# Where the factors' hi and lo parts, the power and a slice's lo part stand in the quads of a Flamingo block kernel

## What is computed

```python
x = x + tanh(g_xattn[0]) * xattn(layernorm(x), ctx, ctx, Wq, Wk, Wv, Wd)   # 32 heads, 8 kv heads, DK = 128, causal
x = x + tanh(g_ffn[0]) * ffn(layernorm(x), ...)

def anemll_linear(x, w, su, sv):       # gate, up (512 -> 1792) and down (1792 -> 512), rank of su @ sv is 4
    w_eff = w * (su @ sv)
    return einsum('bsh,oh->bso', x, w_eff)
# ffn: anemll_linear(silu(gate(x)) * up(x)) for down
```

## Time and profile before

| | us |
|---|---|
| median of 3 runs | 1472.08 (1470.79 to 1472.47) |
| the profiled execution | 1472.51 |
| its span | 1470.7 |
| quads 0 to 43 in the span | about 54 to 510 |
| PE busy in the span | 1451.0 (99%) |

### The profile page before, as it was taken

How to read it: one execution, slowest core, us unless ns; L and a number is a source line. 1 busy time by engine, 2 the same in 40 slices (tenths; PEclk the granted TensorE clock), 3 DMA queues, 4 the chain that set the end, 5 groups by cost and what they waited for, 6 DMA issues and landing times.

```text
span 1470.7 us, 20673 instructions
## 1 busy us (share of the span) xinstructions
PE 1451.0 (99%) x7322; PEld 1185.7 (81%) x7322; DVE 1070.5 (73%) x1578; ACT 642.4 (44%) x1118; POOL 820.2 (56%) x727
## 2 busy tenths in 40 slices
PE   8999999999999999999999999999999999999998
PEld 8878788888888777777777777887888888888887
DVE  5366677877677777767777778777488878767676
ACT  5355454554444343343433444443444444333343
POOL 5598899998888212111111332233388877666664
PEclk9999999999999999999999999999999999999999
DMA  8476677778987644333433334332011121311112
GB/s 274 150 229 210 221 253 250 260 232 291 361 268 265 229 142 140 115 115 134 139 115 115 115 124 155 138 137 65 22 59 50 43 61 48 122 43 59 49 55 75
DMA packets 116070, 218.02 MB, mean 148 GB/s; under 512 B 9472, under 2 KB 47616, under 8 KB 113920
## 3 DMA queue, kind: packets, MB, share of 16 engines
q1 hardware_dynamic: 115968, 216.70, 44.0%
HBM read 151.13 MB, written 65.54 MB: 147 GB/s over the span
## 4 chain that ended last, share of the span: by engine, by line
PE 90%; DVE 5%; issue 1%; DMA 1%; POOL 1%; ACT 1%; SPq 0%; DVEq 0%; ACTq 0%; POOLq 0%
PE bank L543 66%; PE bank L709 4%; PE bank L662 4%; PE bank L845 3%; PE bank L844 3%; PE bank L846 3%; PE bank L671 2%; PE bank L689 2%; DVE el L1265 1%; PE bank L587 1%; DMA c_raw<-in_ctx_t 1%; DVE er L1265 1%; PE bank L742 1%; DVE xc L1259 0%; DMA w_raw<-in_w 0%
## 5 line engine op out<-in xcount | busy, mean ns | idle before, releaser
L1601 POOL TENSOR_TENSOR wd_lo<-wd_raw,wd_hi 128x512 fp32r<-128x512 f32 x64 | 81.9, 1302 | 370.6 <-ACT wd_hi L1011 370.6
L543 PE MATMUL bank<-xc,wa_hi 128*128 128x512 f32 x896 | 277.3, 391 | 0.0
L543 PE MATMUL bank<-wd_hi,o_hi 128*128 128x512 f32 x512 | 202.4, 395 | 0.0
L543 PE MATMUL bank<-wd_hi,o_lo 128*128 128x512 f32 x512 | 199.9, 390 | 0.0
L543 PE MATMUL bank<-wd_lo,o_hi 128*128 128x512 f32 x512 | 199.5, 390 | 0.0
L543 PEld LDWEIGHTS bank<-xc,wa_hi 128*128 128x128 f32 x896 | 167.8, 188 | 35.9 <-issue 1.1
L543 PE MATMUL bank<-xc,wa_lo 128*128 128x512 f32 x448 | 174.5, 390 | 0.0
L1352 DVE TENSOR_TENSOR o_lo<-bank,o_hi 128x512 fp32r<-128x512 f32 x128 | 82.0, 682 | 100.2 <-ACT o_hi L1042 100.2
L1429 DVE SCALAR_TENSOR_TENSOR X<-bank,tg,X 128x512 f32<-128x512 f32 x221 | 154.4, 741 | 0.0
L543 PE MATMUL bank<-x_hi,wf_hi 128*128 128x512 f32 x392 | 153.1, 391 | 0.0
L543 PE MATMUL bank<-x_hi,wf_lo 128*128 128x512 f32 x392 | 152.5, 389 | 0.0
(11 more groups left out here) (180 smaller groups left out, 3411.1 us busy)
## 6 DMA issues: line engine op xcount, KB each, us to landing
q_scratch<-q_st SPq DMA_DIRECT2D x32, 1024.0 KB, 4.3
q_sb<-q_scratch SPq DMA_DIRECT2D x64, 512.0 KB, 5.7
w_raw<-in_wq SPq DMA_DIRECT2D x32, 512.0 KB, 4.0
wd_raw<-in_wd SPq DMA_DIRECT2D x16, 1024.0 KB, 5.1
f_raw<-ffn_eff_scratch SPq DMA_DIRECT2D x28, 512.0 KB, 3.6
er_raw<-in_sf_r SPq DMA_DIRECT2D x42, 256.0 KB, 4.0
e_raw<-in_wf SPq DMA_DIRECT2D x42, 256.0 KB, 5.3
ffn_eff_scratch<-e_eff SPq DMA_DIRECT2D x42, 256.0 KB, 5.1
```

Of the source, the lines that this page charges most:

```text
L543: last = pe.matmul(to, a, b, start=(start and n == 0), stop=(stop and n == 3 * len(pairs) - 1), skip_group_check=onto)
L1601: g.tensor_tensor(wd_lo[h % 2][:, e, :], wd_raw[:, e, :], f32(wd_hi[h % 2][:, e, :]), ALU.subtract).then_inc(g_wd, 1)
```

## The change

Six moves; no instruction is added or taken away, and PE's order is the same.

- ACT: `c_combinations(q + 2)` moves from behind s5 to behind c11.
- ACT: `lr_hi` of quad q+1 is issued at the end of quad q (behind c11), no longer behind s1 of its own quad. Only quad 0 keeps its old place.
- DVE: `lr_lo` likewise moves from behind t1 of its own quad to the end of the quad before, behind `effective`.
- DVE: `x_lo` of a slice moves from the end of quad q to behind t1 (and the moments) of quad q+1.
- POOL: `ln_pow` is issued ahead of `c_combinations_lo` in quads 0 to 7, ahead of `left_sums` in quad 8, and where it was from quad 12 on.
- SP: `load_lr` is issued ahead of `load_w` in a quad.

```diff
--- before.py
+++ after.py
@@ -454,14 +454,14 @@
                 load_e(m)
             if q + 6 < len(LOADS):
                 load_c(q + 6)
+            if q in E_AT and m + 1 < NP:
+                load_lr(m + 1)
             if q in (NV - 4, NV - 3):
                 load_w(q - NV + 4)
             if w == 0:
                 load_w(2)
             if 0 <= w and w + 3 < NW:
                 load_w(w + 3)
-            if q in E_AT and m + 1 < NP:
-                load_lr(m + 1)
             if q in COLUMNS and COLUMNS[q] < 7:
                 load_x(COLUMNS[q] + 1)
 
@@ -971,16 +971,14 @@
             if q:
                 a.wait_ge(v_t2, q)
             a.activation(s1[:, :], bank[0][:, :], ACT.Copy).then_inc(a_s1, 1)
-            if q in E_AT:
-                lr_hi(E_AT[q])
+            if q == 0:
+                lr_hi(0)
             if q in X_SPLIT:
                 x_hi(X_SPLIT[q])
             a.wait_ge(p_p[5], q + 1)
             if q:
                 a.wait_ge(v_c22, q)
             a.activation(s5[:, :], bank[2][:, :], ACT.Copy).then_inc(a_s5, 1)
-            if q + 2 < NCH:
-                c_combinations(q + 2)
             if q == NQ - 1:
                 out_hi(0)
             if q >= NQ - 2:
@@ -997,6 +995,10 @@
             if w >= NK + 2:
                 a.wait_ge(d_qo[w % 2], 16 * ((w - NK) // 2))
             a.activation(result(q, 0, 0), split(q, bank[0][:, :]), ACT.Copy).then_inc(a_c11, 1)
+            if q + 2 < NCH:
+                c_combinations(q + 2)
+            if q + 1 in E_AT:
+                lr_hi(E_AT[q + 1])
             if q in APPLY:
                 apply1(APPLY[q])
 
@@ -1278,10 +1280,12 @@
             v.wait_ge(p_p[6], q + 1)
             v.wait_ge(a_s1, q + 1)
             v.tensor_tensor(t1[:, :], bank[1][:, :], s1[:, :], ALU.add).then_inc(v_t1, 1)
-            if q in E_AT:
-                lr_lo(E_AT[q])
+            if q == 0:
+                lr_lo(0)
             if q in APPLY:
                 ln_moments(APPLY[q])
+            if q - 1 in X_SPLIT:
+                x_lo(X_SPLIT[q - 1])
             if q == NQ - 1:
                 out_lo(0)
             if q >= NQ - 2:
@@ -1310,8 +1314,8 @@
             v.tensor_tensor(result(q, 0, 1), split(q, bank[2][:, :]), split(q, t1[:, :]), ALU.add).then_inc(v_c12, 1)
             if q in E_AT and q < NQ - 2:
                 effective(E_AT[q])
-            if q in X_SPLIT:
-                x_lo(X_SPLIT[q])
+            if q + 1 in E_AT:
+                lr_lo(E_AT[q + 1])
             if q in STATS:
                 stats1(STATS[q])
 
@@ -1688,12 +1692,17 @@
             w = q - NV
             if q + 2 < NCH:
                 c_sums(q + 2)
+            if q < NV and q in APPLY:
+                ln_pow(APPLY[q])
+            if q + 2 < NCH:
                 c_combinations_lo(q + 2)
             if 0 <= w + 1 < NW:
                 left_lo(w + 1)
+            if q == NV and q in APPLY:
+                ln_pow(APPLY[q])
             if 0 <= w + 2 < NW:
                 left_sums(w + 2)
-            if q in APPLY:
+            if q > NV and q in APPLY:
                 ln_pow(APPLY[q])
             if q in COLUMNS:
                 x_sums(COLUMNS[q])
```

## The result

The changed kernel took 1463.89 us (median of 5 runs, 1463.10 to 1465.34), the kernel before 1472.32 (5 runs, 1470.79 to 1472.95). The ratio is 0.9944, with a 95% interval of 0.9934 to 0.9955: 8.2 us faster, from 6.6 to 9.7. The forecast was 1465 in a range of 1460.5 to 1469.

The account below looks back on a forecast made before the run. PE was taken as the bound, busy 1451.0 of 1470.7 us, with 12.8 us of waits or low clock to win; terms -3.8 + 1.2 + 1.4 - 0.6 - 3.8 - 1.7 = -7.3 gave 1465 us, range 1460.5 to 1469.

Parts of the forecast that it names:

- c11 ahead: Quad 0 to 1: copying c11 ahead of the combinations removes PE's idle time and the half clock, gain 3.78 us.
- The new wait in quad 1: Quad 1: PE waits for t1, loss 1.2 us; 0.6 if the first subtraction precedes POOL's long piece, upper bound 1.3.
- The waits for s5 in quads 3 and 6: Quads 3 and 6: combinations behind c11 delay the slice's hi part and s5, 0.7 us each, loss 1.4, bounds 0 and 3.
- The rule of the chain: Quads 2 to 3: combinations to s5 take 10.3 us, so s5 starts at S(3) + 8.0, due S(3) + 8.4, wait 0.7.
- the ruler: Expected time between factors' matmuls, 9.77 us a quad, 10.68 with columns; anything longer counts as lost, 12.8 us in all.
- Quads 4 and 5: Quads 4 and 5: losses fall from 2.14 to 1.5 us, bounds 0.3 and 3, gain 0.6.
- the feared wait of quad 5 for c12: Quad 5: `x_lo` ahead of t2(4) may make t2 some 2 us late and push c12 beyond product 5.
- Power and quads 9 to 12: Quads 8 to 12: power ahead of POOL's sums gains 3.8 us, bounds 2.5 and 5.2; 1.4 us of POOL waits stay.
- Quads 15, 19, 23, 27: Those quads: slice's lo part behind t1 and factors sooner remove the late factors' matmul, gain 1.7 us, bounds 1.2 and 1.7.
- `load_lr` at nothing: SP: `load_lr` ahead of `load_w` costs nothing; factors land ahead of ACT's need, weights two quads ahead are cover enough.
- The rival with a low clock in quad 1: Quad 1's wait lowers the clock, 1.8 us more, and quads 4 to 12 lose 1 to 2: 1468 to 1469, chance 0.14.
- The slower rival: Factors' subtractions delay POOL, so PE waits each quad from 13 on; at 0.6 us a quad about 1483, chance 0.05.

Follow-up runs that it names:

- u_c11: The changed kernel with c11 behind the combinations again in quad 0 alone; 1465.58 us, ratio to the kernel before 0.9960.
- only_c11: The kernel before with one move, c11 ahead of the combinations in quad 0; 1471.45 us, ratio to the kernel before 0.9997.
- comb_q0: The changed kernel with the combinations behind c11 in quad 0 only, behind s5 in the other quads; 1464.67 us, ratio to the kernel before 0.9954.
- xhi_s5: The changed kernel with the slice's hi part behind s5 on ACT, no longer ahead of it; 1463.71 us, ratio to the kernel before 0.9943.
- pow8: The changed kernel with the power back behind the context's lo parts in quads 1, 4 and 6 alone; 1467.80 us, ratio to before 0.9975.
- u_xlo: The changed kernel with the slice's lo part back at the end of its own quad, behind the next factors; 1475.94 us, ratio to before 1.0028.
- u_lr: The changed kernel with the factors' hi and lo parts back in their own quad, behind s1 and t1; 1464.94 us, ratio to before 0.9954.
- u_sp: The changed kernel with the factors' loads behind the weights' loads again; 1523.41 us, ratio to the kernel before 1.0355.

## Why the prediction was right, and where a step was off

- **c11 ahead, 3.78.** Right in what it removed, idle time and low clock both (u_c11). It cannot be had alone (only_c11: 0.4), which the prediction did not see: the others carry it.
- **The new wait in quad 1, 1.2.** 0.61: the lower bound, for the reason given for it. The first subtraction came 0.02 us ahead of the long piece. That was luck; a price that hangs on a few hundredths had better have been given as two cases.
- **The waits for s5 in quads 3 and 6, 0.7 each.** The rule of the chain held: 0.76 and 0.76 on the weight loads, 0.58 on the ruler for quad 6. That they are a net cost is not so clear: taking them away brought little (comb_q0, xhi_s5).
- **Quads 4 and 5, 1.5.** Some 1.15 (the 1.73 less 0.58 for s5 of quad 3), nearly all of it a wait for t1 in quad 4, behind the factors and the statistics; the feared wait of quad 5 for c12 did not come.
- **Power and quads 9 to 12, a gain of 3.8 with 1.4 left.** 5.17 - 0.58 - 1.40 = 3.19, but of the 0.58 all is the wait for s5 counted above, so 3.77 and 1.40. The wait that I named, for POOL's lo parts at the start of quad 11, is there, but it is only 0.35 of the 1.40. The other 1.05 is in quad 12: its start waits for the slice's lo part, which stands behind t1 of quad 11 by another of the moves and took 3.94 us beside POOL's pieces, and then for c12 and t1. And the term missed that the power must be ahead in quads 1 and 4 too, or 4.6 us go (pow8).
- **Quads 15, 19, 23, 27, a gain of 1.7.** 1.7. The reason given, slice's lo part behind t1, needs the factors ahead of t1 as well (u_xlo, u_lr).
- **`load_lr` at nothing.** The step that failed. The changed kernel loses nothing that the ruler shows there (0.03 us in all in quads 13 to 41), but the cover I named, that the factors land ahead of ACT's need, is not there: ACT waits 1.9 us for them. Without the move the factors' new place would have cost 60 us. I had asked what the move costs and not what the change would cost without it.
- The sum, -7.3, against -8.8 in the profiled executions: the difference is the 0.6 in quad 1, 0.2 in the waits for s5, 0.35 in quads 4 and 5, and 0.4 in quad 43, which I had left out.
- The rival with a low clock in quad 1 did not come: the wait there was short, 0.61 on the ruler, and the granted clock stayed at 1.00, from 72 to 74 us too. The slower rival was wrong as put, but what it feared, every quad longer by the same amount with no time to recover, is what u_sp shows, on another path.

## What to carry to other kernels

- In streams in a fixed order, price each move twice: what it costs as made, and what the set costs with this move left out. Here the parts undone one at a time cost 2.4, 1.5, 12.4, 7.5 and 60 us, against 8.2 for the whole.
- A load, a buffer's release and an engine's wait may form a loop. If the wait sits ahead of the work that releases the buffer, the loop has a length of its own; where that is over the length of a round (10.92 against 9.77 us here), every round pays the difference.
- A ruler made of the start times of one matmul per round finds waits that a busy time of 99% hides, and says in which round they are.

## What was not expected of the hardware

- Which of two instructions on the shared SBUF path comes first was decided by 0.02 us (66.77 and 66.79), and changed who was late: the short one took 0.28, the next of DVE 2.77. In the kernel before, 0.07 us the other way cost the short one 2.47. The Trainium skill (SBUF — State Buffer, "Who interferes with whom") says that the order of issue decides which of the two waits; both rows agree.
- The same 1.9 us of idle PE at the same place gave a granted clock of 0.50 in two kernels, before and u_c11. But the length of a wait alone does not tell. Waits of 2.30 us (u_xlo, quad 4) and of 2.43, 1.91 and 2.00 (u_sp) were followed by 0.50 as well; one of 1.65 in quad 9 of the kernel before, of 1.93 in quad 5 of pow8, of 2.06 in u_sp (at 305.90) and of 2.40 in quad 15 of u_xlo left it at 1.00. What decides between them no run here shows. So such a wait has two prices, with the some 1.8 us of low clock behind it and without.
